# Turning rows by VectorE and a DRAM scratch in a conditioned transformer block, and moving weight splits and film products by some steps

## The chip, the cores and the metric

The kernel runs on one core of a Trainium2 chip. The time is that of the device for one execution, in microseconds (us), and lower is better. The core has TensorE (PE, matmuls), VectorE (DVE), ScalarE (ACT), GpSimd (POOL) and SyncE (SP, which only issues DMA transfers here). Each engine works through its own instruction queue in order, and the queues meet only at semaphores.

## The reference

The block has 2 batches of 1024 tokens with 256 features, all in fp32:

```python
def rmsnorm(x, w):
    return x * rsqrt(mean(x * x, -1) + 1e-6) * w
def film(x, cond, w, b):
    scale, shift = split(cond @ w + b, 2)
    return x * (1 + scale) + shift
h = film(rmsnorm(x, norm1_w), cond, film1_w, film1_b)
Q, K, V = h @ q_w + q_b, h @ k_w + k_b, h @ v_w + v_b
x = x + softmax(Q K^T / 16) V @ proj_w + proj_b
h = film(rmsnorm(x, norm2_w), cond, film2_w, film2_b)
return x + gelu(h @ mlp_w1 + mlp_b1) @ mlp_w2 + mlp_b2      # hidden width 1024
```

## The kernel before

**Tiles and groups.** The 2048 tokens are 16 tiles of 128; four tiles are a group, 0 to 3. Rows (`x_rows`) lie with a token per partition. A product needs its left side with a feature per partition; those are the columns `hT`. Each fp32 value is split in a high part (fp32r) and a low part (what is left), and each product is made in three passes (low x high, high x low, high x high). Whatever TensorE multiplies therefore has a high half, made by ScalarE or GpSimd, and a low half, made by VectorE.

**Phase 1** (to about 45 us) loads, makes the first norm and film, turns the rows of each group and makes `G_all` (queries with the key weights folded in) and `V_all` (values with the output projection folded in).

**Phase 2** is attention, one tile a step, `for t in range(TILES)` on each engine. In step t TensorE makes `scores(t)` and then `attention(t - 4)` (`LAG` is 4). VectorE takes the row maximum (L590), turns the probabilities in 32x32 blocks (`turn_blocks`, L601), takes the low half of turned probabilities of tile t - 3 (`crossed_lo`, L608), adds the result of attention to the rows (`add_attention`, L617), and in steps 4 to 11 makes one product for the second film (`film_products`, L477) with the other operand, the condition row, beside it; four products end in `coefficients` (L486, L489) for one batch. ScalarE takes the exponential (`exp`, L386), issues the store of the turned probabilities to a DRAM scratch (`store_turned`, L405) and casts the high half of what came back (`crossed_hi`, L397). SP issues the four loads that bring each tile back with its blocks crossed (L226). `crossed_hi(t)`, then `crossed_lo(t)`, then `attention(t)` is a fixed chain. GpSimd, once `crossed_lo(t)` is done, adds the output bias to the rows of tile t (L305), splits MLP weights (`split_weights`, L292 and L294, one eighth at a time), and adds the second bias (L299).

**The second norm of a group**: squares on ScalarE (`squares_after`, L412), the inverse root on GpSimd (`inverse_rms`, L253 and L256), normed rows on VectorE (`normed_rows`, L497, into `xn`), eight 128x128 transposes on TensorE (`transpose_rows`, L697), film on ScalarE out of PSUM (`columns`, L344), high half on GpSimd (`high_columns`, L261), low half on VectorE (`low_columns`, L511). For group 0 this lies in phase 2.

**Phase 3** is the MLP, one group after the other, eight steps m each: TensorE makes the hidden block m (`hidden`, L705) and the second product of block m - 2 (`project_hidden`, L820); ScalarE takes gelu twice, in fp32 and in fp32r (`gelu_tile`, L446); VectorE takes the low half (`gelu_low`, L653). `finished_rows` (L672) adds the result to the rows, and SP stores them (L234). The transposes for group g + 1 stand in step 4 of group g. The first four hidden blocks of group 0 (`EARLY`) are mixed with the last attentions. Groups 1 and 2 run in a hardware loop (`Fori`) on TensorE, ScalarE and VectorE.

The order is written out by hand in each engine's part, and where the phases meet, ScalarE has this one:

```python
store_turned(TILES - 1)
crossed_hi(TILES - 3)
gelu_tile(0, 0, False)
gelu_tile(0, 1, False)
crossed_hi(TILES - 2)
gelu_tile(0, 2, False)
crossed_hi(TILES - 1)
gelu_tile(0, 3, False)
squares_after(1)
```

## Time and profile before

| | us |
|---|---|
| median of 3 runs (lowest, highest) | 234.83 (233.73, 235.23) |
| the profiled execution | 234.44 |
| its span in the trace | 232.6 |
| TensorE busy in it | 219.7 (94%) |
| VectorE, ScalarE, GpSimd busy | 144.1, 110.7, 71.1 |

The profiled execution's own time is 1.8 us longer than the span from its first to its last instruction. Times in rows count from the span's start. A busy time is a mean over phases: VectorE's 62% is made of a phase 2 that is nearly full and a phase 3 that is not.

### The profile page before, as it was taken

The numbers are of one execution on the slowest core, as the hardware profiler recorded it, in microseconds if no ns is written. First come the engines' busy times: TensorE is split into PE (matmuls) and PEld (weight loads), VectorE is DVE, ScalarE is ACT, GpSimd is POOL, SyncE is SP. The second block draws the span as 40 slices with busy tenths as digits, with TensorE's granted clock in tenths as the row PEclk, the third lists the DMA queues.
The fourth block names the chain that finished last, engine by engine and source line by source line (L and its number), as shares of the span: only waits on it lengthen the run. The fifth ranks groups of instructions, "written<-read, shape, count | busy, mean of one in ns | idle before, by whom it ended". The sixth has DMA issues, their size and how long they took to land.

```text
span 232.6 us, 3855 instructions
## 1 busy us (share of the span) xinstructions
PE 219.7 (94%) x1380; PEld 196.0 (84%) x1380; DVE 144.1 (62%) x276; ACT 110.7 (48%) x207; POOL 71.1 (31%) x102
## 2 busy tenths in 40 slices
PE   0998999999979999999999899999999999999994
PEld 0767988978769999999999799999999999999994
DVE  0599767669599999999879564143524352433223
ACT  3158654425333355423472970367436743644440
POOL 1575851003325513743343224221232123200000
PEclk9999999999999999999999999999999999999999
DMA  6994000054568967665575410000200020002002
GB/s 167 342 368 209 3 19 28 3 180 147 191 222 240 280 215 245 215 211 166 165 239 181 154 30 0 3 0 0 93 0 0 0 90 0 0 4 90 0 3 90
DMA packets 15713, 26.72 MB, mean 115 GB/s; under 512 B 1872, under 2 KB 10064, under 8 KB 15568
## 3 DMA queue, kind: packets, MB, share of 16 engines
q1 hardware_dynamic: 13392, 18.11, 25.2%
q10 hardware_dynamic: 2304, 8.39, 9.4%
q8 instruction: 10, 0.16, 0.3%
q14 instruction: 7, 0.06, 0.1%
HBM read 16.00 MB, written 10.49 MB: 114 GB/s over the span
## 4 chain that ended last, share of the span: by engine, by line
PE 78%; DVE 9%; DMA 6%; issue 2%; SPq 2%; ACT 1%; ACTq 0%; DVEq 0%
PE psum L705 36%; PE psum L820 20%; PE psum L779 16%; DMA raw<-in_film_wT_dram 3%; PE psum L723 3%; DMA crossing<-raw 2%; PE psum L697 2%; PE psum L717 2%; DVE hT L511 1%; DMA keys_first<-crossing 1%; ACT probsT L397 1%; SPq L189 1%; DVE probsT L608 1%; DVE raw L601 1%; DVE V_all L504 1%
## 5 line engine op out<-in xcount | busy, mean ns | idle before, releaser
L653 DVE TENSOR_TENSOR G_all<-probs,G_all 128x512 fp32r<-128x512 f32 x32 | 22.7, 711 | 51.6 <-ACT G_all L446 51.6
L779 PEld LDWEIGHTS psum<-V_all,probsT 128*128 128x128 f32 x384 | 47.1, 188 | 5.1 <-DVE probsT L608 4.2
L820 PEld LDWEIGHTS psum<-w,G_all 128*128 128x128 f32 x384 | 49.6, 191 | 2.1
L820 PE MATMUL psum<-w,G_all 128*128 128x256 f32 x384 | 50.9, 283 | 0.0
L779 PE MATMUL psum<-V_all,probsT 128*128 128x256 f32 x384 | 48.3, 282 | 2.5 <-DVE probsT L608 2.4
L705 PE MATMUL psum<-hT,w 128*128 128x512 f32 (+1 forms) x192 | 49.3, 393 | 0.0
L705 PE MATMUL psum<-hT,G_all 128*128 128x512 f32 x192 | 46.6, 393 | 0.1
L446 ACT ACTIVATE probs<-psum,vcol 128x512 f32<-128x512 f32 x32 | 22.0, 688 | 45.1 <-PE psum L705 45.1
L705 PEld LDWEIGHTS psum<-hT,G_all 128*128 128x128 f32 x192 | 35.1, 188 | 7.7 <-ACT probs L386 0.6
L705 PEld LDWEIGHTS psum<-hT,w 128*128 128x128 f32 x192 | 34.1, 189 | 5.8
L397 ACT CAST probsT<-keys_first 128x1024 fp32r<-128x1024 f32 x16 | 16.8, 1052 | 41.3 <-DVE raw L601 16.6
L305 POOL TENSOR_TENSOR x_rows<-x_rows,add_row 128x256 f32<-128x256 f32 x16 | 11.8, 738 | 69.0 <-DVE probsT L608 69.0
L608 DVE TENSOR_TENSOR probsT<-keys_first,probsT 128x1024 fp32r<-128x1024 f32 x16 | 19.6, 1223 | 6.1 <-ACT probsT L397 5.4
L590 DVE TENSOR_REDUCE row_max<-psum 128x1 f32<-128x1024 f32 x16 | 19.2, 1200 | 5.1 <-PE psum L705 5.1
L446 ACT ACTIVATE G_all<-psum,vcol 128x512 fp32r<-128x512 f32 x32 | 21.9, 683 | 0.0
L386 ACT ACTIVATE probs<-psum,exp_bias 128x1024 f32<-128x1024 f32 x16 | 17.9, 1119 | 7.5 <-DVE exp_bias L593 7.5
L261 POOL TENSOR_SCALAR hT<-h_full 128x512 fp32r<-128x512 f32 x16 | 11.3, 711 | 23.5 <-ACT h_full L344 23.2
L299 POOL TENSOR_TENSOR x_rows<-x_rows,add_row 128x256 f32<-128x256 f32 x16 | 12.9, 828 | 11.1 <-DVE xn L497 11.1
L511 DVE TENSOR_TENSOR hT<-h_full,hT 128x512 fp32r<-128x512 f32 (+1 forms) x16 | 11.4, 744 | 3.0 <-POOL hT L261 3.0
L705 PE MATMUL psum<-probsT,hT 128*128 128x258 f32 x96 | 12.4, 285 | 0.0
L344 ACT ACTIVATE h_full<-psum,coef 128x512 f32<-128x512 f32 x16 | 11.6, 778 | 1.8 <-DVE coef L489 1.2
L705 PEld LDWEIGHTS psum<-probsT,hT 128*128 128x128 f32 x96 | 11.9, 189 | 0.1
(63 smaller groups left out, 198.7 us busy)
## 6 DMA issues: line engine op xcount, KB each, us to landing
keys_first<-crossing SPq DMA_DIRECT2D x64, 128.0 KB, 3.0
crossing<-turned ACTq DMA_DIRECT2D x8, 512.0 KB, 4.1
crossing<-raw ACTq DMA_DIRECT2D x8, 512.0 KB, 3.4
out_dram<-x_rows SPq DMA_DIRECT2D x8, 256.0 KB, 2.1
x_rows<-in_x_dram SPq DMA_DIRECT2D x3, 512.0 KB, 9.4
raw<-in_film_wT_dram SPq DMA_DIRECT2D x2, 512.0 KB, 8.5
raw<-in_mlp_w_dram SPq DMA_DIRECT2D x1, 1024.0 KB, 7.6
raw<-in_mlp_w_dram SPq DMA_DIRECT2D x4, 256.0 KB, 4.6
```

What stands on the lines that cost most here:

```text
L299: pool.tensor_tensor(row, row, add_row[:, 1, :], ALU.add).then_inc(bias2_added, 1)
L305: pool.tensor_tensor(x_rows[:, t, :], x_rows[:, t, :], add_row[:, 0, :], ALU.add).then_inc(residual_ready, 1)
L386: act.activation(probs[:, parity, :], psum[:, 2 * parity:2 * parity + 2, :].rearrange("p a n -> p (a n)"), ACT.Exp, bias=exp_bias[:, t:t + ...
L397: act.copy(probsT[:, t % 2, HI, :, :].rearrange("p k (a n) -> p k a n", n=Q), keys_first[:, t % 2, :, :, :].rearrange("p a k n -> p k a n" ...
L446: act.activation(dst, bank(2 + m % 2), ACT.Gelu, bias=vcol[:, B1 + m:B1 + m + 1]).then_inc(gelu_done, 1)
L511: dve.tensor_tensor(hT[:, LO, d, tokens], h_full[:, d, :], hT[:, HI, d, tokens].bitcast(F32), ALU.subtract).then_inc(h_ready, 1)
L590: dve.reduce_max(row_max[:, col], psum[:, 2 * parity:2 * parity + 2, :].rearrange("p a n -> p (a n)"), AX_X, negate=True).then_inc(max_don ...
L608: dve.tensor_tensor(lo, keys_first[:, t % 2, :, :, :].rearrange("p a k n -> p k a n"), hi.bitcast(F32), ALU.subtract).then_inc(probsT_read ...
L653: dve.tensor_tensor(gelu[:, m, LO, :], gelu_full[:, m % 2, :], gelu[:, m, HI, :].bitcast(F32), ALU.subtract).then_inc(gelu_ready, 1)
L705: last = pe.matmul(dst, stationary(a, k), moving(b, k), start=(n == len(tiles) * len(PASSES) - 1), stop=(n == 0))
L779: last = pe.matmul(bank(6 + t % 2, D), probsT[:, t % 2, a, k, :], V_all[:, t // KT * KT + k, s, :], start=(n == 0), stop=(n == KT * len(PA ...
L820: last = pe.matmul(bank(4 + j, D), gelu[:, m, a, j * P:(j + 1) * P], w2[:, b, m, :], start=(m == 0 and n == 0), stop=(m == HT - 1 and n == ...
```

## The change

1. **Rows of groups 1 to 3 are turned without TensorE.** A new `turn_rows(g)` on VectorE turns `xn` in 32x32 blocks into `turned_rows`. `cross_rows(g)` on SP stores this 512 KB to the scratch `rows_crossing` and loads it back in four pieces with the blocks crossed, into `columns_first`. ScalarE's `columns_after` reads that instead of PSUM. Group 0 is turned by TensorE as before.
2. **The places of this work.** The squares of group 1 stand right behind ScalarE's last `store_turned`; norm and turn of group 1 stand on VectorE ahead of `crossed_lo(15)`. Those of groups 2 and 3 are in step 0 of the group before, ahead of `finished_rows`, with the squares in step 6 of the group before that.
3. **The weight splits** on GpSimd go from steps 0 to 3 and 6 to 9 to steps 4 to 7 and 10 to 13, and SP's loads of the second weights from steps 5 to 8 to steps 9 to 12. `turned_rows` and `columns_first` lie in the memory of the raw weights. TensorE waits for four pieces ahead of its first hidden block and for all eight ahead of the rest.
4. **The film products** on VectorE go from steps 4 to 11 to steps 5 to 8 (one each), 9 and 10 (two each).
5. The `Fori` loops of phase 3 are written out.

```diff
+        rows_crossing = nc.dram_tensor("rows_crossing", [GROUPS, P, GT * D], F32)
...
+        turned_rows = raw[:, 0:GT * D]
+        columns_first = raw[:, GT * D:2 * GT * D].rearrange("p (a d j n) -> p a d j n", a=QT, d=DT, j=GT)
...
+        rows_turned, rows_out, columns_in = sem("rows_turned"), sem("rows_out"), sem("columns_in")
...
             for t in range(TILES):
-                if 5 <= t < 9:
-                    sp.wait_ge(mlp_ready, t - 4)
-                    load(w2_raw[:, (t - 5) * 512:(t - 4) * 512].rearrange("p (t n) -> p t n", n=D),
-                         mlp_w2[:, (t - 5) * 2:(t - 4) * 2, :], w2_in[t - 5])
+                if 9 <= t < 13:
+                    sp.wait_ge(mlp_ready, t - 8)
+                    load(w2_raw[:, (t - 9) * 512:(t - 8) * 512].rearrange("p (t n) -> p t n", n=D),
+                         mlp_w2[:, (t - 9) * 2:(t - 8) * 2, :], w2_in[t - 9])
                 sp.wait_ge(turned_out, 16 * (t + 1))
...
-            with sp.Fori(0, B) as b:
-                for t in range(0, KT, 2):
-                    sp.wait_ge(rows_done, b * KT + (TILES + t + 2))
-                    sp.dma_start(out_v[:, ds(b, 1), t:t + 2, :].rearrange("p b t n -> p (b t) n"),
-                                 x_rows[:, ds(b * KT + t, 2), :]).then_inc(stored, 16)
+            def cross_rows(g):
+                sp.wait_ge(rows_turned, g)
+                sp.dma_start(rows_crossing[g, :, :], turned_rows).then_inc(rows_out, 16)
+                sp.wait_ge(rows_out, 16 * g)
+                sp.wait_ge(h_done, DT * (GROUPS + g))
+                for q in range(QT):
+                    sp.dma_start(
+                        columns_first[q * Q:(q + 1) * Q, :, :, :, :].rearrange("p a d j n -> p a (d j n)"),
+                        rows_crossing[g, :, q * GT * DT * Q:(q + 1) * GT * DT * Q].rearrange("(a p) n -> p a n", p=Q),
+                    ).then_inc(columns_in, 16)
+
+            def store_rows(g):
+                b, first = divmod(g * GT, KT)
+                for j in range(0, GT, 2):
+                    sp.wait_ge(rows_done, TILES + g * GT + j + 2)
+                    sp.dma_start(out_v[:, b, first + j:first + j + 2, :],
+                                 x_rows[:, g * GT + j:g * GT + j + 2, :]).then_inc(stored, 16)
+
+            cross_rows(1)
+            cross_rows(2)
+            store_rows(0)
+            cross_rows(3)
+            for g in range(1, GROUPS):
+                store_rows(g)
             sp.wait_ge(stored, 16 * TILES // 2)

         @block.gpsimd
...
-                    pool.wait_ge(w2_in[t - 6], 16)
-                    split_weights(w2_raw, w2_flat, t - 6, 4)
+                if 4 <= t < 8:
+                    split_weights(w1_raw, w1_flat, t - 4, 0)
+                if 10 <= t < 14:
+                    pool.wait_ge(w2_in[t - 10], 16)
+                    split_weights(w2_raw, w2_flat, t - 10, 4)
                 if t == 6:
...
@@ -318,9 +341,12 @@
                     second_bias(t - 10)
                 if t == 11:
                     high_columns(GROUPS, 0)
+                if t == 13:
+                    inverse_rms(GROUPS + 1)

             for g in range(1, GROUPS):
-                inverse_rms(g + GROUPS)
+                if g > 1:
+                    inverse_rms(g + GROUPS)
                 pool.wait_ge(xn_done, TILES + GT * (g + 1))
                 for j in range(GT):
...
@@ -407,16 +433,27 @@
             def squares_after(g, tiles=range(GT), place=lambda j: xn[:, j, :]):

                 act.wait_ge(rows_done, g * GT + GT)
-                act.wait_ge(xT_done, g + GROUPS)
+                if g <= 1:
+                    act.wait_ge(xT_done, g + GROUPS)
+                else:
+                    act.wait_ge(rows_turned, g - 1)
                 for j in tiles:
                     last = act.activation(place(j), x_rows[:, ds(g * GT + j, 1), :].rearrange("p t n -> p (t n)"),
                                           ACT.Square, accum_out=sumsq[:, ds(g * GT + (TILES + j), 1)])
                 if GT - 1 in tiles:
                     last.then_inc(sq_done, 1)

-            def columns_after(g, first=0):
+            def columns_after(g):
                 act.wait_ge(h_ready, g * DT + DT * GROUPS)
-                columns(g + GROUPS, 1, ds(g // 2, 1), first)
+                if g == 0:
+                    columns(GROUPS, 1, slice(0, 1), 4)
+                else:
+                    act.wait_ge(columns_in, 16 * QT * g)
+                    for d in range(DT):
+                        act.activation(h_full[:, d, :].rearrange("p (j a n) -> p j a n", j=GT, a=QT),
+                                       columns_first[:, :, d, :, :].rearrange("p a j n -> p j a n"), ACT.Identity,
+                                       bias=coef[:, 1, g // 2, DT + d:DT + d + 1],
+                                       scale=coef[:, 1, g // 2, d:d + 1]).then_inc(h_done, 1)

             squares_place = [h_full[:, 0, D:2 * D], h_full[:, 1, 0:D], h_full[:, 1, D:2 * D], xn[:, GT - 1, :]]
             high_V(GROUPS - 1, range(2))
...
@@ -447,6 +484,7 @@
                                    ).then_inc(gelu_done, 1)

             store_turned(TILES - 1)
...
@@ -454,20 +492,17 @@
             gelu_tile(0, 2, False)
             crossed_hi(TILES - 1)
             gelu_tile(0, 3, False)
-            squares_after(1)
-
-            def mlp(g, before, more):
-                for m in range(0 if before else EARLY, HT):
-                    gelu_tile(g, m, before)
-                    if more and m == 0:
-                        squares_after(g + 1)
-                    if more and m == 5:
+
+            def mlp(g):
+                for m in range(0 if g else EARLY, HT):
+                    gelu_tile(g, m, g > 0)
+                    if m == 5 and g + 1 < GROUPS:
                         columns_after(g + 1)
-
-            mlp(0, False, True)
-            with act.Fori(1, GROUPS - 1) as g:
-                mlp(g, True, True)
-            mlp(GROUPS - 1, True, False)
+                    if m == 6 and g + 2 < GROUPS:
+                        squares_after(g + 2)
+
+            for g in range(GROUPS):
+                mlp(g)

         @block.vector
...
+
+            def turn_rows(g):
+
+                dve.wait_ge(xn_done, TILES + GT * (g + 1))
+                dve.wait_ge(mlp_ready, 8)
+                if g > 1:
+                    dve.wait_ge(rows_out, 16 * (g - 1))
+                dve.transpose(turned_rows.rearrange("p (q d j n) -> p d j q n", q=QT, d=DT, j=GT),
+                              xn[:, :, :].rearrange("p j (d q n) -> p d j q n", d=DT, q=QT)).then_inc(rows_turned, 1)

...
                     add_attention(t - LAG)
-                if LAG <= t < LAG + 2 * DT * B:
-                    b, k = divmod(t - LAG, 2 * DT)
-                    if t == LAG:
+                if 5 <= t < 9:
+                    if t == 5:
                         dve.wait_ge(film_in[1], 16)
                         dve.wait_ge(wide_in, 32)
-                    film_products(1, b, lambda n: h_full[:, 0, 0:D], (k,))
-                    if k == 2 * DT - 1:
-                        coefficients(1, b)
+                    film_products(1, 0, lambda n: h_full[:, 0, 0:D], (t - 5,))
+                    if t == 8:
+                        coefficients(1, 0)
+                if t in (9, 10):
+                    film_products(1, 1, lambda n: xn[:, 2, :] if n % 2 else h_full[:, 0, 0:D], (2 * t - 18, 2 * t - 17))
+                    if t == 10:
+                        coefficients(1, 1)
                 if t in (TILES - 5, TILES - 4):
                     normed_rows(GROUPS, 0, range(2) if t == TILES - 5 else range(2, GT))
...
@@ -658,11 +705,12 @@
             crossed_lo(TILES - 2)
             add_attention(TILES - 3)
             gelu_low(0, 2)
+            normed_rows(GROUPS + 1, GT)
+            turn_rows(1)
             crossed_lo(TILES - 1)
             add_attention(TILES - 2)
             gelu_low(0, 3)
             add_attention(TILES - 1)
-            normed_rows(GROUPS + 1, GT)

             def finished_rows(g):
                 for j in range(GT):
...
+                        normed_rows(g + (GROUPS + 1), g * GT + GT)
+                        turn_rows(g + 1)
+                    if m == 0:
                         finished_rows(g - 1)
-                    if more and m == 2:
-                        normed_rows(g + (GROUPS + 1), g * GT + GT)
-                    if more and m == 6:
-                        low_columns(g + (GROUPS + 1), ds(g * GW + GW, GW))
-
-            mlp(0, False, True)
-            with dve.Fori(1, GROUPS - 1) as g:
-                mlp(g, True, True)
-            mlp(GROUPS - 1, True, False)
+                    if m == 6 and g + 1 < GROUPS:
+                        low_columns(g + (GROUPS + 1), slice(g * GW + GW, g * GW + 2 * GW))
+
+            for g in range(GROUPS):
+                mlp(g)
             finished_rows(GROUPS - 1)

...
@@ -822,22 +869,20 @@
                     if m == HT - 1:
                         last.then_inc(mlp_done, 1)

-            def mlp(g, before, more):
+            def mlp(g, before):

...
-                    if more and m == 4:
-                        transpose_rows(g + (GROUPS + 1))
                     if m >= 2:
                         project_hidden(g, m - 2, before)
                     elif before:
                         project_hidden(g - 1, HT - 2 + m)

             attention(TILES - 4)
-            pe.wait_ge(mlp_ready, 8)
+            pe.wait_ge(mlp_ready, 4)
...
@@ -847,10 +892,9 @@
             hidden(0, 3)
             attention(TILES - 2)
             attention(TILES - 1)
-            mlp(0, False, True)
...
-            mlp(GROUPS - 1, True, False)
+            pe.wait_ge(mlp_ready, 8)
+            for g in range(GROUPS):
+                mlp(g, g > 0)
             for m in (HT - 2, HT - 1):
                 project_hidden(GROUPS - 1, m)


```

**ScalarE where phase 2 ends.** The `DMA` row is the store of turned probabilities of tile 15, `CAST` is `crossed_hi`, first of tile 13, `ACTIVATE xn,sumsq` is a square. Before:

```order
L405 DMA crossing<-raw 128x1024 [waits turned_out,blocks_turned]
L397 CAST probsT<-keys_first 128x1024 [waits attn_done,keys_in_odd]
L446 ACT_TABLE_LOAD [waits blocks_turned]
L446 ACTIVATE probs<-psum,vcol 128x512 [waits hidden_done]
L446 ACTIVATE G_all<-psum,vcol 128x512
...
L397 CAST probsT<-keys_first 128x1024 [waits attn_done,keys_in_odd]
L446 ACTIVATE probs<-psum,vcol 128x512 [waits gelu_ready,hidden_done]
L446 ACTIVATE G_all<-psum,vcol 128x512
L412 ACTIVATE xn,sumsq<-x_rows 128x256 [waits xT_done,rows_done]
```

Now:

```order
L431 DMA crossing<-raw 128x1024 [waits turned_out,blocks_turned]
L441 ACTIVATE xn,sumsq<-x_rows 128x256 [waits xT_done,rows_done]
L441 ACTIVATE xn,sumsq<-x_rows 128x256 x3
L423 CAST probsT<-keys_first 128x1024 [waits attn_done,keys_in_odd]
L483 ACT_TABLE_LOAD [waits blocks_turned]
L483 ACTIVATE probs<-psum,vcol 128x512 [waits hidden_done]
L483 ACTIVATE G_all<-psum,vcol 128x512
```

The squares have gone from behind the fourth gelu to ahead of the cast of tile 13 and of all four gelus.

**VectorE at the same meeting of phases.** `probsT<-keys_first,probsT` is `crossed_lo`, here of tile 15, `G_all` is `gelu_low`, `xn<-x_rows` the normed rows of group 1. Before:

```order
L653 TENSOR_TENSOR G_all<-probs,G_all 128x512 [waits gelu_done]
L608 TENSOR_TENSOR probsT<-keys_first,probsT 128x1024 [waits probsT_hi]
L614 RECIPROCAL row_inv<-row_sum 128x1 [waits attn_done]
L617 SCALAR_TENSOR_TENSOR x_rows<-psum,row_inv,x_rows 128x256 [waits residual_ready,inv_done]
L653 TENSOR_TENSOR G_all<-probs,G_all 128x512 [waits gelu_done]
L614 RECIPROCAL row_inv<-row_sum 128x1 [waits attn_done]
L617 SCALAR_TENSOR_TENSOR x_rows<-psum,row_inv,x_rows 128x256 [waits residual_ready,inv_done]
L497 TENSOR_SCALAR xn<-x_rows,rstd 128x256 [waits rstd_done]
L497 TENSOR_SCALAR xn<-x_rows,rstd 128x256 x3
L653 TENSOR_TENSOR G_all<-probs,G_all 128x512 [waits gelu_done] x3
```

Now:

```order
L700 TENSOR_TENSOR G_all<-probs,G_all 128x512 [waits gelu_done]
L532 TENSOR_SCALAR xn<-x_rows,rstd 128x256 [waits rstd_done]
L532 TENSOR_SCALAR xn<-x_rows,rstd 128x256 x3
L541 STREAM_TRANSPOSE raw<-xn 128x8x4x32 [waits mlp_ready,xn_done]
L652 TENSOR_TENSOR probsT<-keys_first,probsT 128x1024 [waits probsT_hi]
L658 RECIPROCAL row_inv<-row_sum 128x1 [waits attn_done]
L661 SCALAR_TENSOR_TENSOR x_rows<-psum,row_inv,x_rows 128x256 [waits residual_ready,inv_done]
L700 TENSOR_TENSOR G_all<-probs,G_all 128x512 [waits gelu_done]
L658 RECIPROCAL row_inv<-row_sum 128x1 [waits attn_done]
L661 SCALAR_TENSOR_TENSOR x_rows<-psum,row_inv,x_rows 128x256 [waits residual_ready,inv_done]
```

The normed rows have gone from behind the last `add_attention` to ahead of `crossed_lo(15)`, and the new turn of `xn` stands between.

**VectorE in step 10.** `h_full,film_sum<-raw,xn` is a film product, followed by the read of its sum. Before:

```order
L614 RECIPROCAL row_inv<-row_sum 128x1 [waits attn_done]
L617 SCALAR_TENSOR_TENSOR x_rows<-psum,row_inv,x_rows 128x256 [waits residual_ready,inv_done]
L477 ISA h_full,film_sum<-raw,xn 128x256
L477 ISA film_sum 128x1
L601 STREAM_TRANSPOSE turned<-probs 128x8x4x32 [waits turned_out,exp_done]
L590 TENSOR_REDUCE row_max<-psum 128x1 [waits scores_done]
```

Now:

```order
L658 RECIPROCAL row_inv<-row_sum 128x1 [waits attn_done]
L661 SCALAR_TENSOR_TENSOR x_rows<-psum,row_inv,x_rows 128x256 [waits residual_ready,inv_done]
L512 ISA h_full,film_sum<-raw,xn 128x256
L512 ISA film_sum 128x1
L512 ISA xn,film_sum<-raw,xn 128x256
L512 ISA film_sum 128x1
L521 TENSOR_TENSOR coef<-film_sum,vcol 128x4 [waits film_sums]
L524 SCALAR_TENSOR_TENSOR coef<-coef,vcol 128x2 [waits shift_ready]
L645 STREAM_TRANSPOSE turned<-probs 128x8x4x32 [waits turned_out,exp_done]
L634 TENSOR_REDUCE row_max<-psum 128x1 [waits scores_done]
```

Where one product stood there are two, with the coefficients of the second batch behind them, all ahead of the turn of tile 10.

## Rows read from the trace of the kernel before

**Rows 1.** The page: engines, busy; a gelu pass: count, busy, mean ns.

```profile
PE 219.7 (94%) x1380; PEld 196.0 (84%) x1380; DVE 144.1 (62%) x276; ACT 110.7 (48%) x207; POOL 71.1 (31%) x102
...
L446 ACT ACTIVATE probs<-psum,vcol 128x512 f32<-128x512 f32 x32 | 22.0, 688 | 45.1 <-PE psum L705 45.1
```

**Rows 2.** Chain of waits, whole span: start us, length us, what.

```profile
63.69 3.14 DMA crossing<-raw
...
109.27 2.84 PE psum L779 x24
...
130.65 3.11 PE psum L779 x24
...
136.52 5.68 PE psum L779 x48
...
146.46 0.87 PE psum L697 x8
...
193.34 0.87 PE psum L697 x8
```

**Rows 3.** Timeline, TensorE (PE), 60 to 232.6 us: start, length, instruction [idle before <-releaser].

```profile
103.49 3.00 PE L779 MATMUL psum<-V_all,probsT 128*128 128x256 f32 x24
...
130.65 3.11 PE L779 MATMUL psum<-V_all,probsT 128*128 128x256 f32 x24 [0.65 <-DVE probsT L608]
...
164.09 1.60 PE L820 MATMUL psum<-w,G_all 128*128 128x256 f32 x12
```

**Rows 4.** Timeline, ScalarE (ACT), 96 to 175 us.

```profile
127.86 0.33 ACTq L405 DMA_DIRECT2D crossing<-raw  x1
128.28 1.05 ACT L397 CAST probsT<-keys_first 128x1024 fp32r<-128x1024 f32 x1 [4.10 <-DVE raw L601]
...
138.43 0.43 ACT L412 ACTIVATE xn<-x_rows 128x256 f32<-128x256 f32 x1
...
139.62 0.42 ACT L412 ACTIVATE xn<-x_rows 128x256 f32<-128x256 f32 x1
```

**Rows 5.** Timeline, VectorE (DVE), 96 to 175 us.

```profile
126.59 1.23 DVE L601 STREAM_TRANSPOSE raw<-probs 128x1024 f32<-128x1024 f32 x1
129.37 1.23 DVE L608 TENSOR_TENSOR probsT<-keys_first,probsT 128x1024 fp32r<-128x1024 f32 x1 [1.54 <-ACT probsT L397]
...
137.41 1.23 DVE L608 TENSOR_TENSOR probsT<-keys_first,probsT 128x1024 fp32r<-128x1024 f32 x1 [0.24 <-ACT probsT L397]
...
142.83 1.14 DVE L497 TENSOR_SCALAR xn<-x_rows,rstd 128x256 f32<-128x256 f32 x4
```

**Rows 6.** Timeline, VectorE, 60 to 110 us.

```profile
64.14 1.43 DVE L477 CUSTOM_DVE_ANT_0 h_full<-raw,xn 128x256 f32<-128x256 f32 x1
...
96.12 0.58 DVE L477 CUSTOM_DVE_ANT_0 h_full<-raw,xn 128x256 f32<-128x256 f32 x1
...
98.08 1.23 DVE L590 TENSOR_REDUCE row_max<-psum 128x1 f32<-128x1024 f32 x1 [0.20 <-PE psum L705]
...
99.53 1.22 DVE L608 TENSOR_TENSOR probsT<-keys_first,probsT 128x1024 fp32r<-128x1024 f32 x1
...
101.97 0.45 DVE L486 TENSOR_TENSOR coef<-film_sum,vcol 128x4 f32<-128x4 f32 x1
```

**Rows 7.** Timeline, GpSimd (POOL), 50 to 110 us.

```profile
63.99 1.30 POOL L294 TENSOR_TENSOR w<-raw,w 128x512 fp32r<-128x512 f32 x1
...
96.40 0.80 POOL L292 TENSOR_SCALAR w<-raw 128x512 fp32r<-128x512 f32 x1
97.28 1.30 POOL L294 TENSOR_TENSOR w<-raw,w 128x512 fp32r<-128x512 f32 x1
```

**Rows 8.** Timeline, VectorE, 160 to 175 us.

```profile
161.94 1.50 DVE L672 TENSOR_TENSOR x_rows<-psum,x_rows 128x256 f32 x4 [1.20 <-PE psum L820]
```

**Rows 9.** The page: DMA issues, count, KB each, median us to landing.

```profile
keys_first<-crossing SPq DMA_DIRECT2D x64, 128.0 KB, 3.0
...
crossing<-raw ACTq DMA_DIRECT2D x8, 512.0 KB, 3.4
```

14 lines of the change are left out of this document (5 added, 9 removed).

## The prediction

> **What bounds the kernel now.** I read the page first: TensorE is busy 94% of the span, VectorE 62%, the others less [rows 1]. Then the chain of waits: from 69.7 us to 229.6 us it stays on TensorE but for one piece, around 125 to 130 us. There attention of the fourteenth tile (tile 13) starts after 0.65 us of idle time, released by VectorE's low half of the turned probabilities (L608) [rows 2, 3]. A stretch of eight 128x128 transposes stands in that chain with 0.87 us each time; those for groups 1 and 3 are at 146.46 and 193.34 [rows 2], with group 2's midway. So whatever leaves TensorE's queue after 70 us is a gain, provided its queue never waits for a new reason. VectorE matters next: between 50 and 100 us it has almost no gap, and it hands TensorE one tile at a time.
>
> The profiled execution took 234.44 us (span 232.6). The median of the shown runs is 234.83. My sums are against 234.44, 0.4 us under that median, which is small beside the terms.
>
> **Term 1, the transposes of groups 1 to 3.** 3 x 0.87 = **-2.6 us**, all of it on the path. TensorE now also waits for all eight weight pieces only after attention of tile 15, and for four before its first hidden matmul. By rows the first four are split by about 100 us; nothing is won or lost by it.
>
> **Term 2, the squares of group 1 on ScalarE.** Four Square instructions, 0.40 us apart (138.43 to 140.0) [rows 4], stand today behind the last early gelu, where ScalarE has time. Now they stand right behind ScalarE's last store of turned rows and ahead of the cast of tile 13 (L397). What is queued behind them is the critical piece: VectorE's turn ends at 127.8, ScalarE issues the store at 127.86, casts at 128.28, VectorE takes the low half at 129.37, TensorE starts at 130.65 [rows 3 to 5]. ScalarE is in order and is idle before 127.86, waiting for that turn, so the squares cannot run earlier. The cast moves to 129.88 and TensorE's wait grows from 0.65 to 2.25: **+1.6 us**. Bounds: 1.5 to 1.7, since the same instructions were timed.
>
> **Term 3, norm and turn of group 1 on VectorE.** Its four row products (1.14) [rows 5] and a new 32x32 block turn of 128x1024 now stand ahead of the low half of tile 15. The turn has the shape of today's L601, 1.23 [rows 5]. Together 2.37. Today that low half runs at 137.41 to 138.64, after 0.24 idle, and attention of tile 15 starts 2.84 into the 48 matmuls at 136.52, that is 139.36: slack 0.72 [rows 2, 5]. Everything here has moved by the 1.6 of term 2 alike, so the slack stays. 2.37 less 0.24, less some 0.1 by which neighbours overlap, gives 2.0; less 0.72 is 1.3 us of stall. A restart of TensorE costs more: attention takes 3.11 after a wait and 2.84 without [rows 2], 0.27. Together **+1.6 us**. The products need the inverse norm from GpSimd, which now has in step 13 a residual, a weight split (0.7 to 0.8 and 1.30 [rows 7]), a bias and the two norm instructions: by today's durations it is done between 137 and 139.4, wanted at 138.7. So the bounds are 1.0 (half the overlap I assume is missing) and 2.5 (norm 0.7 late and slow).
>
> **Term 4, film products on VectorE.** The eight move from steps 4 to 11 to steps 5 to 8 (one each), 9 and 10 (two each). Step 4 loses one of 1.43 us [rows 6]; nothing comes of it, because ScalarE next needs the store issued at 63.69 to land at 66.83 [rows 2] before it can go on. Step 11 loses its product, its coefficients and their quarrel with GpSimd. The price lies in steps 9 and 10. A product runs today at 96.12 beside GpSimd's residual and ends at 96.70; GpSimd's L292 has then begun and ends at 97.20, L294 (1.30) follows [rows 6, 7]. The trace shows that such pairs exclude each other: the product issued at 64.14 took 1.43 where another took 0.58, because L294 was in progress since 63.99, and it ended 0.28 after L294 [rows 6, 7]. The second product, issued at 96.65 in these terms, waits to 97.20, ends at about 97.5: 0.86 more than today. Twice that, 1.7. The coefficients leave step 7 (-0.4), come to step 8 (+0.7, as at 101.97, where the first took 0.45 [rows 6]) and to step 10, where the first would find L294 in progress: 1.4, or 0.4 if it slips in. Less the 0.2 that VectorE idles before 98.08, the maximum of tile 11 is 3.3 us later (2.3 if it slips in). TensorE bears 2.7: attention of tile 8 starts at 103.49, its low half ends today at 100.75 [rows 3, 6]. So the stall is 0.6 plus 0.27 for the restart, **+0.8 us**; the lower bound is 0. Steps 11 and 12 then have only two row products each and step 13 nothing added, so I take VectorE to be abreast again by step 14, as it was at 98.08.
>
> What the notes add: the Trainium skill ("SBUF — State Buffer", Who interferes with whom) says that a VectorE instruction with two SBUF inputs and a GpSimd instruction that reads SBUF exclude each other for the whole instruction, whichever issues first going first. That is what the product at 64.14 shows (1.43 instead of 0.58). The rule does not say who goes next when both wait; read with L294 issued first it would make term 4 3.4 in place of 0.8, which is rival (c) below.
>
> **At nothing.** The weight splits, 2 us each on GpSimd, go from steps 0 to 3 and 6 to 9 to steps 4 to 7 and 10 to 13. GpSimd idles several us a step there. The high columns of group 0 come some 2 us later behind a split, at about 123.3, and VectorE wants them at 124.84; if that cover were gone, each us late would be a us of TensorE. The round trip of a group through DRAM: store 3.4, four loads issued in 1.7 and landed 3.0 later [rows 9], together some 8 us, plus the turn. A step of the MLP is (46.88 - 2 x 0.87) / 16 = 2.82, from the transposes of groups 1 and 3 [rows 2]. In times of today's group 1, VectorE is free at 160.74 (161.94 less 1.20), so norm and turn of group 2 end at 163.1 [rows 8]. ScalarE wants the columns behind its gelu of the sixth hidden block, whose matmuls end three steps after 164.09, at 172.5, and two passes of 0.69 later it is 173.9 [rows 1, 3]. The columns are there at 163.1 + 8.1 = 171.2: 2.7 us of cover, and the same for group 3. Group 1 has about 4. SP issues these ahead of the output stores, which nobody waits for but the last. In the same place VectorE's finished rows (1.50 for four) come behind norm and turn: they would start at about 163.1 in place of 161.94 and end at 164.6, and TensorE needs the first at 164.09 and the last 1.1 later [rows 3, 8]: just in time, zero, up to 0.3 each. The loops written out cost and save nothing, as TensorE shows no gap at them.
>
> **Sum.** -2.6 + 1.6 + 1.6 + 0.8 = +1.4, so **235.8 us**. With the bounds of terms 3 and 4 the forecast's own range is 234.4 to 236.8.
>
> **Rivals.**
> (a) The change simply gains: the tail waits are hidden, and the time is 234.4 - 2.6 = 231.8. For it: TensorE is the bound nearly everywhere. Against it: [rows 3 to 5] show no slack before tile 13's cast, and ScalarE is in order. 10%.
> (b) Only one of the two tail waits counts and VectorE holds its pace: -2.6 + 1.6 + 0 to 0.8, that is 233.4 to 234.2. It needs the low half of tile 15 to find 2 us of cover that I do not see, or none of term 4. 17%.
> (c) Slower: the shared access of VectorE and GpSimd. If L294 goes ahead of the second product in steps 9 and 10, each costs 1.3 more. The maximum of tile 11 is then 5.9 late instead of 3.3, and TensorE waits 3.1 + 0.27. Decisive point: that maximum later than 100.8. The sum is -2.6 + 1.6 + 1.6 + 3.4 = +4.0, 238.4. For it: L294 is issued 0.08 after L292 ends [rows 7]. Against it: in today's rows the one that waited went next. 14%.
> (d) The change doesn't deliver: the round trip takes twice its 8 us beside other transfers, the columns come 5 us late in groups 2 and 3, and TensorE, which has one step of 2.8 in hand, loses 2.5 in each: 241. The DMA queues are nearly empty there, so 4%.
> The forecast has the remaining 55%.
>
> **How the numbers follow.** A measurement of this kernel tells about 1% from no change, 2.3 us. Faster by more than that is (a) and the very edge of (b): 0.12. Slower is (c), (d) and a little of the forecast's upper end: 0.20. The rest, 0.68, is within 1%. The range 233.0 to 238.2 leaves out (a), (d) and the upper part of (c).
>
> **What the changed profile would show.** Term 1: no L697 transposes of groups 1 to 3, and TensorE without a gap from about 146 us to the end. Term 2: four squares between the last store and the cast of tile 13, and an idle of about 2.2 us before that attention. Term 3: an idle of 1 to 2 us before attention of tile 15, released by VectorE's low half. Term 4: second film products of about 0.9 and a small idle near 104 us. I am wrong if TensorE shows no idle time between 120 and 146 us beyond today's, or waits inside the MLP groups for columns or finished rows.

## The result, and the profile after

| | before | after |
|---|---|---|
| median, us (4 runs each) | 235.03 (233.73 to 235.58) | 237.57 (236.92 to 238.21) |
| profiled execution, us | 234.44 | 237.56 |
| its span, us | 232.6 | 235.5 |

The ratio is 1.0100, with a 95% interval of 1.0063 to 1.0137: slower, by about the 1% that a measurement of this kernel can tell. Three of the four executions of the changed kernel, the profiled one among them, had a mean granted TensorE clock of 0.993 and spans of 235.5 to 235.6 us. The fourth had 1.000 and 234.2. The forecast span was 232.6 + 1.4 = 234.0.

In the experiments below the medians and the counts of executions are of all of them, and the ratios leave out one of e1_squares_first (237.75) and one of s1_before_squares_late (239.68), each over 1.5% longer than the fastest of its kernel.

The page of the changed kernel: engines, busy time, and the DMA issues of the new round trip. TensorE has 24 matmuls less than in [rows 1].

```profile
PE 219.0 (93%) x1356; PEld 194.6 (83%) x1356; DVE 148.4 (63%) x279; ACT 110.8 (47%) x207; POOL 73.1 (31%) x102
...
rows_crossing<-raw SPq DMA_DIRECT2D x3, 512.0 KB, 2.6
raw<-rows_crossing SPq DMA_DIRECT2D x12, 128.0 KB, 2.9
```

The timeline of TensorE in the changed kernel, as in [rows 3]: start, length, instruction, idle time before it with its releaser. L826 is attention, L752 the hidden matmuls, L867 the projections.

```profile
98.20 3.00 PE L826 MATMUL psum<-V_all,probsT 128*128 128x256 f32 x24
...
109.63 3.00 PE L826 MATMUL psum<-V_all,probsT 128*128 128x256 f32 x24
...
124.97 3.11 PE L826 MATMUL psum<-V_all,probsT 128*128 128x256 f32 x24 [0.24 <-DVE probsT L652]
127.91 2.94 PE L752 MATMUL psum<-hT,w 128*128 128x512 f32 x12
133.24 4.62 PE L826 MATMUL psum<-V_all,probsT 128*128 128x256 f32 x24 [2.38 <-DVE probsT L652]
137.70 2.93 PE L752 MATMUL psum<-hT,w 128*128 128x512 f32 x12
140.47 3.00 PE L826 MATMUL psum<-V_all,probsT 128*128 128x256 f32 x24
144.77 3.11 PE L826 MATMUL psum<-V_all,probsT 128*128 128x256 f32 x24 [1.31 <-DVE probsT L652]
147.72 2.55 PE L867 MATMUL psum<-w,G_all 128*128 128x256 f32 x20
...
228.11 4.47 PE L867 MATMUL psum<-w,G_all 128*128 128x256 f32 x36
```

The waits before tile 13 (2.38) and tile 15 (1.31) are the two that terms 2 and 3 forecast. The third thing to see is the length 4.62 at 133.24: the same 24 matmuls took 3.11 after a wait before [rows 3].

The same stretch of the changed kernel in windows of 1 us; the third figure from the right is the granted clock, ahead of DMA share and GB/s.

```profile
133.00:134.00 1.00, 0.76 (x4) 0.77 (x5) 0.74 (x3) 0.99 (x3) 0.74 (x2) 0.76 0.00 0
134.00:135.00 1.00, 1.00 (x7) 1.00 (x6) 0.46 (x1) 1.00 (x3) 0.92 (x2) 0.50 0.46 134
...
136.00:137.00 1.00, 1.00 (x7) 1.00 (x7) 1.00 (x2) 0.59 (x1) 1.00 (x2) 0.54 0.52 118
137.00:138.00 1.00, 1.00 (x10) 0.95 (x9) 1.00 (x1) 0.00 (x0) 0.92 (x2) 1.00 0.00 0
```

TensorE was idle from 130.85 to 133.24. The granted clock then stands at 0.50, its 1.2 GHz level, from about 133.5 to 136.9, with 7 matmuls a microsecond in place of 10.

Starts on TensorE before and after, in the order of time, give the whole shift. The last column is what the prediction had for the same stretch.

| TensorE reaches | before | after | shift | new here | forecast here |
|---|---|---|---|---|---|
| attention of tile 7 | 97.88 | 98.20 | +0.32 | +0.32 | 0 |
| attention of tile 9 | 109.10 | 109.63 | +0.53 | +0.21 | +0.8 (term 4) |
| hidden block 0 of group 0 | 127.07 | 127.91 | +0.84 | +0.31 | 0 ("at nothing") |
| attention of tile 13 | 130.65 | 133.24 | +2.59 | +1.75 | +1.6 (term 2) |
| hidden block 2 | 133.59 | 137.70 | +4.11 | +1.52 | 0 |
| attention of tile 14 | 136.36 | 140.47 | +4.11 | 0 | 0 |
| first projection | 142.03 | 147.72 | +5.69 | +1.58 | +1.6 (term 3) |
| last 36 matmuls | 225.07 | 228.11 | +3.04 | -2.65 | -2.6 (term 1) |

The first +0.32 stands in the trace from 56 us on, ahead of everything that the prediction costs. s1_before_squares_late below, whose code is that of before up to 128 us, reaches its hidden block 0 at 127.40, 0.33 late as well, so I take it for the scatter of executions.

ScalarE of the changed kernel, to be read against [rows 4]: the four squares (L441) between the last store and the cast of tile 13 (L423).

```profile
128.85 0.33 ACTq L431 DMA_DIRECT2D crossing<-raw  x1
129.28 0.42 ACT L441 ACTIVATE xn<-x_rows 128x256 f32<-128x256 f32 x1 [4.57 <-DVE raw L645]
...
130.50 0.40 ACT L441 ACTIVATE xn<-x_rows 128x256 f32<-128x256 f32 x1
...
130.90 1.03 ACT L423 CAST probsT<-keys_first 128x1024 fp32r<-128x1024 f32 x1
```

The cast starts 1.62 after the place that the first square took.

VectorE of the changed kernel, against [rows 5, 6]: film products (L512), coefficients (L521), the maximum of tile 11 (L634), low halves (L652), low columns (L555), low half of a gelu (L700), norm (L532) and turn (L541) of group 1.

```profile
91.96 0.82 DVE L512 CUSTOM_DVE_ANT_0 xn<-raw,xn 128x256 f32<-128x256 f32 x1
...
98.62 1.12 DVE L521 TENSOR_TENSOR coef<-film_sum,vcol 128x4 f32<-128x4 f32 x1
...
101.03 1.18 DVE L634 TENSOR_REDUCE row_max<-psum 128x1 f32<-128x1024 f32 x1
...
123.38 1.53 DVE L652 TENSOR_TENSOR probsT<-keys_first,probsT 128x1024 fp32r<-128x1024 f32 x1
...
125.42 2.24 DVE L555 TENSOR_TENSOR hT<-h_full,hT 128x512 fp32r<-128x512 f32 x2
...
131.96 1.23 DVE L652 TENSOR_TENSOR probsT<-keys_first,probsT 128x1024 fp32r<-128x1024 f32 x1 [3.14 <-ACT probsT L423]
...
135.69 1.23 DVE L700 TENSOR_TENSOR G_all<-probs,G_all 128x512 fp32r<-128x512 f32 x1 [0.47 <-ACT G_all L483]
136.84 1.75 DVE L652 TENSOR_TENSOR probsT<-keys_first,probsT 128x1024 fp32r<-128x1024 f32 x1
...
141.19 1.14 DVE L532 TENSOR_SCALAR xn<-x_rows,rstd 128x256 f32<-128x256 f32 x4
142.37 1.25 DVE L541 STREAM_TRANSPOSE raw<-xn 128x1024 f32<-128x1024 f32 x1
143.53 1.18 DVE L652 TENSOR_TENSOR probsT<-keys_first,probsT 128x1024 fp32r<-128x1024 f32 x1
```

And GpSimd of the changed kernel beside it, as in [rows 7]: high columns (L284), second halves of weight splits (L317) and an addition of the second bias (L322).

```profile
92.59 1.34 POOL L317 TENSOR_TENSOR w<-raw,w 128x512 fp32r<-128x512 f32 x1
...
121.27 1.29 POOL L317 TENSOR_TENSOR w<-raw,w 128x512 fp32r<-128x512 f32 x1
...
123.22 2.17 POOL L284 TENSOR_SCALAR hT<-h_full 128x512 fp32r<-128x512 f32 x2
...
127.21 1.61 POOL L317 TENSOR_TENSOR w<-raw,w 128x512 fp32r<-128x512 f32 x1
...
134.66 1.71 POOL L317 TENSOR_TENSOR w<-raw,w 128x512 fp32r<-128x512 f32 x1
136.33 1.18 POOL L322 TENSOR_TENSOR x_rows<-x_rows,add_row 128x256 f32<-128x256 f32 x1
```

The low half of 1.53 in place of 1.23 stands where GpSimd runs its high columns. At 134.66 the split runs beside a gelu's low half, which takes 1.23 in place of 0.69, and the bias addition that the split has pushed back runs beside the low half of 1.75. Both sides are slowed: L317 takes 1.61 beside the low columns and 1.71 beside the gelu, 1.29 at 121.27, and L322 takes 1.18 in place of 0.74.

### The profile page after: what moved, and what is told of

Same layout as the page of the kernel before. It is cut to its first block, busy times and chain, and to the rows that moved or that the text cites. A ratio compares the mean times of both kernels' runs of the same rounds, so it can differ in the third digit from the quotient of the medians.

```text
span 235.5 us, 3657 instructions
## 1 busy us (share of the span) xinstructions
PE 219.0 (93%) x1356; PEld 194.6 (83%) x1356; DVE 148.4 (63%) x279; ACT 110.8 (47%) x207; POOL 73.1 (31%) x102
## 4 chain that ended last, share of the span: by engine, by line
PE 74%; DVE 11%; DMA 7%; issue 3%; ACT 2%; SPq 2%; ACTq 0%; DVEq 0%
PE psum L752 35%; PE psum L867 19%; PE psum L826 14%; DMA raw<-in_film_wT_dram 3%; PE psum L770 2%; DMA crossing<-raw 2%; DVE probsT L652 2%; PE psum L764 1%; DMA keys_first<-crossing 1%; ACT probsT L423 1%; DVE hT L555 1%; PE psum L744 1%; SPq L193 1%; DVE row_max L634 1%; DVE raw L645 1%
## 5 line engine op out<-in xcount | busy, mean ns | idle before, releaser
L826 PEld LDWEIGHTS psum<-V_all,probsT 128*128 128x128 f32 x384 | 48.6, 194 | 9.0 <-DVE probsT L652 8.3
L826 PE MATMUL psum<-V_all,probsT 128*128 128x256 f32 x384 | 50.2, 288 | 5.8 <-DVE probsT L652 5.8
L700 DVE TENSOR_TENSOR G_all<-probs,G_all 128x512 fp32r<-128x512 f32 x32 | 23.4, 730 | 51.0 <-ACT G_all L483 51.0
L867 PEld LDWEIGHTS psum<-w,G_all 128*128 128x128 f32 x384 | 49.8, 191 | 2.3
L867 PE MATMUL psum<-w,G_all 128*128 128x256 f32 x384 | 50.6, 283 | 0.0
L752 PE MATMUL psum<-hT,w 128*128 128x512 f32 x192 | 49.3, 393 | 0.0
L752 PE MATMUL psum<-hT,G_all 128*128 128x512 f32 x192 | 46.5, 393 | 0.1
L752 PEld LDWEIGHTS psum<-hT,G_all 128*128 128x128 f32 x192 | 35.1, 188 | 7.6 <-ACT probs L412 0.6
L752 PEld LDWEIGHTS psum<-hT,w 128*128 128x128 f32 x192 | 34.1, 189 | 5.8
L423 ACT CAST probsT<-keys_first 128x1024 fp32r<-128x1024 f32 x16 | 16.8, 1049 | 38.8 <-DMA keys_first<-crossing 10.6
L328 POOL TENSOR_TENSOR x_rows<-x_rows,add_row 128x256 f32<-128x256 f32 x16 | 11.8, 739 | 70.7 <-DVE probsT L652 70.7
L652 DVE TENSOR_TENSOR probsT<-keys_first,probsT 128x1024 fp32r<-128x1024 f32 x16 | 20.4, 1275 | 9.1 <-ACT probsT L423 8.4
L284 POOL TENSOR_SCALAR hT<-h_full 128x512 fp32r<-128x512 f32 x16 | 12.2, 768 | 37.4 <-ACT h_full L453 28.7
L634 DVE TENSOR_REDUCE row_max<-psum 128x1 f32<-128x1024 f32 x16 | 19.2, 1198 | 4.4 <-PE psum L752 4.4
L322 POOL TENSOR_TENSOR x_rows<-x_rows,add_row 128x256 f32<-128x256 f32 x16 | 12.3, 793 | 8.8 <-DVE xn L532 8.8
L555 DVE TENSOR_TENSOR hT<-h_full,hT 128x512 fp32r<-128x512 f32 x16 | 11.8, 769 | 3.0 <-POOL hT L284 3.0
L752 PE MATMUL psum<-probsT,hT 128*128 128x258 f32 x96 | 12.4, 285 | 0.0
L752 PEld LDWEIGHTS psum<-probsT,hT 128*128 128x128 f32 x96 | 11.9, 189 | 0.1
L317 POOL TENSOR_TENSOR w<-raw,w 128x512 fp32r<-128x512 f32 x8 | 11.1, 1394 | 0.7
```

The source lines that it names most:

```text
L284: pool.tensor_scalar(hT[:, HI, d, g * GW:(g + 1) * GW], h_full[:, d, :], 1.0, 0.0, ALU.mult, ALU.add).then_inc(h_hi, 1)
L322: pool.tensor_tensor(row, row, add_row[:, 1, :], ALU.add).then_inc(bias2_added, 1)
L423: act.copy(probsT[:, t % 2, HI, :, :].rearrange("p k (a n) -> p k a n", n=Q), keys_first[:, t % 2, :, :, :].rearrange("p a k n -> p k a n" ...
L555: dve.tensor_tensor(hT[:, LO, d, tokens], h_full[:, d, :], hT[:, HI, d, tokens].bitcast(F32), ALU.subtract).then_inc(h_ready, 1)
L634: dve.reduce_max(row_max[:, col], psum[:, 2 * parity:2 * parity + 2, :].rearrange("p a n -> p (a n)"), AX_X, negate=True).then_inc(max_don ...
L652: dve.tensor_tensor(lo, keys_first[:, t % 2, :, :, :].rearrange("p a k n -> p k a n"), hi.bitcast(F32), ALU.subtract).then_inc(probsT_read ...
```

## The experiments

Ten kernels, each timed against the kernel before in turn on one chip: e1, e2, e3 and s1 together (before 234.68), f1, f3, s2 and e4 together (235.13), f2 and e5 together (235.11). All of them compute the whole reference. Diffs are against the kernel named.

**Squares ahead of the last store (e1_squares_first, from after).**

```diff
-            store_turned(TILES - 1)
             squares_after(1)
+            store_turned(TILES - 1)
             crossed_hi(TILES - 3)
```

> The changed kernel with one swap: on ScalarE the four squares of group 1 stand ahead of the last store of turned rows instead of behind it, that is in the 4 us in which ScalarE waits for VectorE's turn anyway. Theory (term 2): the wait of TensorE before attention of tile 13 falls from 2.38 to about 0.8 us, and the fall of the granted clock behind it (that attention took 4.62 instead of 3.11 us) goes too; the changed kernel loses 3.1 us, to about 234.4. Rival A (the loss comes from the moved weight splits and film products, which make VectorE late): the cast still comes late and less than 1 us returns. Rival B (the clock falls for a reason other than this wait): 1.6 us return and that attention still takes over 4 us.

Measured: 235.69 (12 runs), ratio 1.0022 [0.9998, 1.0046]. TensorE's timeline:

```profile
131.45 3.10 PE L826 MATMUL psum<-V_all,probsT 128*128 128x256 f32 x24 [0.79 <-DVE probsT L652]
...
142.08 4.63 PE L826 MATMUL psum<-V_all,probsT 128*128 128x256 f32 x24 [1.96 <-DVE probsT L652]
```

The squares ran at 124.6 to 126.2, where ScalarE waits for VectorE's turn anyway, and the wait before tile 13 fell from 2.38 to 0.79. So term 2 is the place of the squares; 0.14 of that wait is something else. By the medians 1.9 us came back, where 3.1 was expected. The wait before tile 15 became 1.96, not 1.31, and now that attention took 4.63. Windows of this kernel across it:

```profile
140.00:142.00 2.00, 0.12 (x2) 0.00 (x0) 2.00 (x3) 0.00 (x0) 0.00 (x0) 1.00 0.12 49
142.00:146.00 4.00, 3.92 (x20) 3.92 (x21) 1.35 (x4) 0.00 (x0) 3.89 (x5) 0.57 0.53 186
```

In the profiled execution the drop of the clock moved with the long wait, from tile 13 to tile 15.

**The squares alone, in the kernel before (s1_before_squares_late, from before).**

```diff
             store_turned(TILES - 1)
+            squares_after(1)
             crossed_hi(TILES - 3)
...
             gelu_tile(0, 3, False)
-            squares_after(1)
```

> The kernel before, with only this moved: the squares of group 1 on ScalarE stand behind the last store of turned rows, ahead of the cast of tile 13, as in the changed kernel. Theory (term 2 with the clock): TensorE's wait there grows from 0.65 to 2.25 us and the attention behind it takes about 4.6 us: 3.1 us slower than before, about 238. Rival B: 1.6 us slower, with that attention at 3.1 us.

Measured: 236.94 (6 runs), ratio 1.0071 [1.0047, 1.0096], 1.7 us. TensorE:

```profile
132.57 4.62 PE L779 MATMUL psum<-V_all,probsT 128*128 128x256 f32 x24 [2.25 <-DVE probsT L608]
```

The wait is the 2.25 of term 2, to the hundredth, and nothing of the rest of the change is in this kernel. The 1.7 us are by the ratio; the median of all six executions is 2.3 over that of before. The profiled execution has the lower clock behind the wait (mean 0.991, span 236.1), and the longest of the others has a low mean clock too (0.990, span 237.9); the remaining four have not (0.997 to 0.999, spans 234.2 to 235.7). So the time is 1.6 for the wait, and the sum of wait and clock that I had expected is reached by those two executions, not by the ratio.

**Half of the squares late (s2_two_squares_late, from before).**

```diff
+            squares_after(1, range(2))
             store_turned(TILES - 1)
+            squares_after(1, range(2, GT))
             crossed_hi(TILES - 3)
```

> The kernel before, with two of the four squares of group 1 ahead of ScalarE's last store and two behind it, ahead of the cast of tile 13. Theory: the wait of TensorE there is 0.65 + 0.8 = 1.45 us, 0.8 us slower than before, and the granted clock holds, so the attention behind it takes 3.1 us. Rival E (any wait over 1 us costs the clock): that attention takes about 4.6 us and the kernel is 2.3 us slower.

Measured: 235.98 (10 runs), ratio 1.0030 [1.0013, 1.0047], 0.7 us.

```profile
132.51 3.11 PE L780 MATMUL psum<-V_all,probsT 128*128 128x256 f32 x24 [1.47 <-DVE probsT L609]
```

Two squares add 0.82 to the 0.65 and leave attention at 3.11. The mean clock was 0.997 or more in all ten executions. The cost of squares in front of the cast is linear, 0.4 each.

**e1 with the weight splits and their loads back in the steps of before (f3_e1_old_splits, from e1).**

```diff
-                if 4 <= t < 8:
-                    split_weights(w1_raw, w1_flat, t - 4, 0)
-                if 10 <= t < 14:
-                    pool.wait_ge(w2_in[t - 10], 16)
-                    split_weights(w2_raw, w2_flat, t - 10, 4)
+                if t < 4:
+                    split_weights(w1_raw, w1_flat, t, 0)
+                if 6 <= t < 10:
+                    pool.wait_ge(w2_in[t - 6], 16)
+                    split_weights(w2_raw, w2_flat, t - 6, 4)
```

SP's loads of w2 go back from tiles 9 to 12 to tiles 5 to 8 in the same way.

> The kernel of e1 (squares in ScalarE's idle time) with the weight splits and loads back in their old steps. Theory (GpSimd's share of term 3): in e1 the low half of tile 14 took 1.75 and the normed rows 1.61 us beside GpSimd's split and norm, against 1.23 and 1.14 without; both go, and the wait at tile 15 falls from 1.96 to 1.2 or 1.3 us, near the 1.3 of the prediction. With it the clock holds in more executions. Median 1.5 to 2 us under e1. Rival: the wait stays at 1.9 and so does the time.

Measured: 234.22 (12 runs), ratio 0.9966 [0.9950, 0.9982]. TensorE, then VectorE in the same trace:

```profile
104.26 3.11 PE L826 MATMUL psum<-V_all,probsT 128*128 128x256 f32 x24 [0.52 <-DVE probsT L652]
...
131.49 3.10 PE L826 MATMUL psum<-V_all,probsT 128*128 128x256 f32 x24 [0.65 <-DVE probsT L652]
...
141.50 3.11 PE L826 MATMUL psum<-V_all,probsT 128*128 128x256 f32 x24 [1.31 <-DVE probsT L652]
```

```profile
134.88 1.23 DVE L652 TENSOR_TENSOR probsT<-keys_first,probsT 128x1024 fp32r<-128x1024 f32 x1 [0.24 <-ACT probsT L423]
...
137.93 1.14 DVE L532 TENSOR_SCALAR xn<-x_rows,rstd 128x256 f32<-128x256 f32 x4
```

With the split gone the low half is at 1.23 again, and the wait at tile 15 is the 1.3 that term 3 worked out from norm and turn alone. e1's other 0.65 came with the split of step 13 and what it pushed back on GpSimd: there the gelu's low half took 1.24, the low half of tile 14 1.75 beside the bias addition, and the normed rows 1.61, against 0.69, 1.23 and 1.14 here. The clock was 0.998 or more in all 12 executions. By the ratios the gain on e1 is 1.3 us, where 1.5 to 2 was expected.

**Only the splits back (f1_only_old_splits, from after).** The same edit, with after's squares:

```diff
-                if 4 <= t < 8:
+                if t < 4:
...
-                if 10 <= t < 14:
+                if 6 <= t < 10:
```

> The changed kernel with only the weight splits and the loads of the second weights back in the steps of the kernel before. Theory (GpSimd's reads hold up VectorE in steps 12 to 15): the wait of 0.24 at tile 12 goes (0.5 us with its restart), the two low columns take 1.8 instead of 2.24, so the cast of tile 13 is 0.4 earlier by itself; the squares stay in front of it, so the wait there stays at 2.2 us. 0.5 to 1.0 us faster than the changed kernel. Rival A: 2 us or more.

Measured: 236.81 (4 runs), ratio 1.0075 [1.0052, 1.0098]; 0.8 under after, with intervals that overlap. TensorE's rows:

```profile
127.35 2.92 PE L752 MATMUL psum<-hT,w 128*128 128x512 f32 x12
132.52 3.11 PE L826 MATMUL psum<-V_all,probsT 128*128 128x256 f32 x24 [2.25 <-DVE probsT L652]
```

The wait at tile 12 is gone. The hidden block starts 0.56 earlier than in after, but 0.25 of that stands ahead of tile 11 already (121.48 against 121.73), so 0.31 came back with the wait, which is the table's +0.31. The wait at tile 13 is 2.25 again. This profiled execution kept the clock (1.000, span 233.3); the three others had 0.993 and 234.8 to 235.3. One kernel, two kinds of execution, some 1.5 to 2 us apart.

**Only the film products back (f2_only_old_film, from after).**

```diff
-                if 5 <= t < 9:
...
-                if t in (9, 10):
...
+                if LAG <= t < LAG + 2 * DT * B:
+                    b, k = divmod(t - LAG, 2 * DT)
```

> The changed kernel with only the film products back in steps 4 to 11, one each. Theory (term 4 is 0.2 us, as the first trace after the change shows at tile 8): 0.1 to 0.4 us faster than the changed kernel, the waits at tiles 13 and 15 as they are. Rival A (VectorE's load of steps 9 and 10 is the main loss): over 1 us faster.

Measured: 236.98 (5 runs), ratio 1.0079 [1.0049, 1.0109]. Beside after's interval this tells nothing apart; waits of 2.02 and 1.92 at tiles 13 and 15, and a clock of 0.993 in three of five executions. What term 4 cost shows in the traces better than in the times. From attention of tile 7 to that of tile 9 TensorE took:

| film products | us from tile 7 to tile 9 |
|---|---|
| old steps: before, f2, e3, e4, e5, s1 | 11.21 to 11.23 |
| old steps: s2 | 11.69 |
| new steps: after, e1, e2, f1, f3 | 11.43, 11.48, 11.49, 11.59, 11.99 |

So the new steps cost 0.2 to 0.4 in four executions and 0.8 in f3. s2 has 0.5 there without them: ScalarE's cast waited for the loads from DRAM until 100.44. The old steps can be late by chance, but only the new ones are late every time.

**Norm and turn behind the last early gelu (e2_norm_behind, from e1).**

```diff
-            normed_rows(GROUPS + 1, GT)
-            turn_rows(1)
             crossed_lo(TILES - 1)
             add_attention(TILES - 2)
             gelu_low(0, 3)
+            normed_rows(GROUPS + 1, GT)
+            turn_rows(1)
             add_attention(TILES - 1)
```

> The swap of e1, and on VectorE norm and turn of group 1 moved from ahead of the low half of tile 15 to behind the low half of the fourth gelu. Theory (term 3): TensorE's wait of 1.31 us before attention of tile 15 goes with its restart, another 1.6 us, so about 232.8. The turned rows leave about 2 us later and their columns still come in time. Rival C (the low half of tile 15 would be late anyway, by the keys from DRAM): under 0.4 us returns. Rival D (columns late): a new wait of TensorE at the first hidden block of group 1.

Measured: 233.34 (5 runs), ratio 0.9928 [0.9907, 0.9948]. The wait before tile 15 is gone and one of 0.36 is new, in the first projection, released by VectorE's `add_attention`, which now stands behind the turn. Both tail waits taken away, the change gains.

**The old splits and film products as well (e3_old_splits, from e2).** The edits of f3 and f2 together:

```diff
-                if 4 <= t < 8:
+                if t < 4:
...
-                if 5 <= t < 9:
+                if LAG <= t < LAG + 2 * DT * B:
```

> e2, with weight splits, loads of the second weights and film products in the steps of the kernel before. What is left of the change is the turn by VectorE and DRAM for groups 1 to 3. Theory: the stall of 0.2 at tile 8 and that of 0.24 at tile 12 (its low half, 1.53 instead of 1.23, beside GpSimd's high columns) go with their restarts, 0.5 to 0.8 us, so about 232.1, 2.6 to 2.9 us under the kernel before. Rival A would have it 2 us faster than e2.

Measured: 233.19 (6 runs), ratio 0.9931 [0.9905, 0.9957]. The wait at tile 12 is gone and tile 13's is 0.65, and the profiled span is 0.8 shorter (230.7 against 231.5), but the medians differ by 0.15 and the ratios not at all. The gain I expected is not there in the times.

**The turn behind the last attention sum (e4_turn_last, from e3).**

```diff
             normed_rows(GROUPS + 1, GT)
-            turn_rows(1)
             add_attention(TILES - 1)
+            turn_rows(1)
```

> The kernel of e3 with one swap on VectorE: the addition of attention of tile 15 stands between the norm and the turn of group 1 instead of behind both. Theory: the last small wait of TensorE there (0.37 us and its restart, released by that addition) goes, 0.4 us, so 0.2% faster than e3; the columns of group 1 come 1.1 us later and are still in time. Rival D (columns late): ScalarE waits for them, and TensorE has a new wait of up to 1 us before the first hidden block of group 1.

Measured: 233.10 (6 runs), ratio 0.9915 [0.9888, 0.9942]. The wait in the first projection went and another came:

```profile
156.73 1.65 PE L749 MATMUL psum<-hT,w 128*128 128x512 f32 x6 [0.25 <-DVE hT L555]
```

The columns of group 1, whose turn starts at 142.96 instead of 142.04 in e3, now miss the first hidden block of group 1: rival (d) in small, at the one group that the prediction gave about 4 us of cover.

**Norm and turn each in a gap (e5_norm_in_gap, from e4).** The norm goes behind the turn of tile 15, where VectorE waits for ScalarE's cast (1.54 of idle, [rows 5]), and the turn ahead of the last sum. GpSimd's inverse norm of group 1 comes at step 12.

```diff
-                if t == 13:
+                if t == 12:
                     inverse_rms(GROUPS + 1)
...
+            normed_rows(GROUPS + 1, GT)
             crossed_lo(TILES - 3)
...
             gelu_low(0, 3)
-            normed_rows(GROUPS + 1, GT)
-            add_attention(TILES - 1)
             turn_rows(1)
+            add_attention(TILES - 1)
```

> The kernel of e4 with norm and turn of group 1 in gaps of VectorE: the inverse norm on GpSimd one step earlier, the four row products behind the turn of tile 15, where VectorE waits 1.5 us for ScalarE's cast, and the turn of the rows ahead of the last addition, where it waits again. Theory: all of it is covered, the columns come 1 us earlier than in e4 and its wait of 0.3 us at the first hidden block of group 1 goes, so 0.2 to 0.4 us under e4, about 2.6 us under the kernel before. Rival F (the row products don't fit: GpSimd's norm is late): VectorE waits ahead of the low half of tile 13 and TensorE's wait there grows from 0.65 towards 1.5 us.

Measured: 232.02 (6 runs, 231.81 to 232.37), ratio 0.9868 [0.9845, 0.9892]. VectorE, then TensorE:

```profile
126.92 1.23 DVE L645 STREAM_TRANSPOSE raw<-probs 128x1024 f32<-128x1024 f32 x1
128.19 1.14 DVE L532 TENSOR_SCALAR xn<-x_rows,rstd 128x256 f32<-128x256 f32 x4
129.69 1.23 DVE L652 TENSOR_TENSOR probsT<-keys_first,probsT 128x1024 fp32r<-128x1024 f32 x1 [0.35 <-ACT probsT L423]
...
140.94 1.23 DVE L541 STREAM_TRANSPOSE raw<-xn 128x1024 f32<-128x1024 f32 x1
```

```profile
130.97 3.11 PE L823 MATMUL psum<-V_all,probsT 128*128 128x256 f32 x24 [0.67 <-DVE probsT L652]
...
136.65 5.84 PE L823 MATMUL psum<-V_all,probsT 128*128 128x256 f32 x48
...
222.73 4.47 PE L864 MATMUL psum<-w,G_all 128*128 128x256 f32 x36
```

The norm fills 1.14 of the idle time and the low half still waits 0.35 for the cast. TensorE waits 0.67, as before the change, and has no wait behind it. The last matmuls start at 222.73, 2.34 before those of before: term 1 with nothing given back but the scatter. It is the fastest of all kernels here, 1.3% under the kernel before and 2.3% under the change as made (0.9868 / 1.0100).

## Why the prediction was right, and where it fell short

It forecast +1.4 us, and the medians are 2.5 apart: 237.57 lies inside the stated range of 233.0 to 238.2, but 0.8 above the 236.8 that the bounds of its own terms allowed. It is also nearer to rival (c)'s 238.4 than to the forecast of 235.8, though (c)'s mechanism did not act. So the direction and the three new costs were foreseen, the clock's share was not, and that the time fell inside the range owes something to the width that was left for (c). The terms:

- **Term 1, -2.6: right.** 2.65 between the first projection and the last 36 matmuls, and e5 shows it by itself.
- **Term 2, +1.6: right as to cause and size.** s1 holds nothing but these squares and has the wait of 2.25, s2 has half of it, e1 takes it away. After has 0.13 more; its low columns took 2.24 beside GpSimd, 1.83 in f1.
- **What term 2 lacked is what stood behind the wait.** The prediction gave a wait its own length and 0.27 for the restart. At tile 13 attention itself took 4.62 instead of 3.11, with the granted clock at 0.50: +1.52 in the profiled execution, the largest miss, and most of the 1.8 us between forecast and median. What a fall costs in the end is nearer 1.4: after's spans are 235.5 to 235.6 with it and 234.2 in the one execution without, where the sum gives 234.0.
- **Term 3, +1.6: right as to cause, and in its size two misses cancel.** f3 shows norm and turn by themselves: a wait of 1.31, and 0.27 of restart. Beside the split of step 13, with the clock kept, the wait is 1.96 (e1) or 1.92 (f2): 0.6 that I did not have. In after's profiled execution 1.31 stands there again: VectorE stood idle 1.39 before 140.59, until the late hidden block and its gelu were done, so the slow attention of tile 13 hid the delay. The norm from GpSimd, my upper bound, was not last in after: it ended at 139.77 and the normed rows started at 141.19. In e1 it was level with VectorE: it ended at 138.00, the gelu's low half at 138.02, and the rows started at 138.03.
- **Term 4, +0.8: right as to cause, mis-sized; it was 0.2 in after.** Each second product kept VectorE 0.75 (91.96 to 92.71) where I had 0.86, and the first coefficient instruction 1.12 where I had 1.4 or 0.4. With the 0.32 of the whole trace taken off, the maximum of tile 11 was 2.6 later, between my 2.3 and 3.3, and TensorE bears 2.7. But the margin is thin: the same instructions made that maximum 3.2 late against TensorE in f3, and there the wait was 0.52 and the price 0.8, as forecast. VectorE had less lead there before the first product of step 10 (97.57 with tile 7's attention at 97.98; 97.24 and 98.20 in after), and why is open.
- **"At nothing" failed in one place: the high columns of group 0.** I looked at when they would be ready for VectorE's low columns and put that at 123.3, 1.5 us early. Pushed behind the split they only began at 123.22, beside VectorE's low half of tile 12. The two took 2.17 in place of 1.22 and ended at 125.39, 0.03 ahead of the low columns, and the low half took 1.53 and came 0.24 late for TensorE. f1 gives the 0.31 at the hidden block back. No data came late, but the cover was used up, and the price was paid by the engine beside it. The other items held: the round trip (2.6 for the store; loads 2.9) was in time for groups 2 and 3, and no wait stands in the MLP.
- **The rivals.** (a), the change simply gains, was wrong for the code as made, and right for its idea: e2 and e5 gain as soon as the two tail waits are gone. (b) needed one of them hidden, and neither was. (c), GpSimd's second half ahead of the film products, did not come about: L317 began at 92.59 and 98.39, behind the issue of the second products at 91.96 and 97.76. Its decisive point, a maximum later than 100.8, was badly chosen. It is only where TensorE's cover ends, and the forecast's own 3.3 lies past it too, so after's 101.03 passes it without (c). (d) did not either; e4 shows where it begins.

So in after's trace misses stand on both sides: 0.6 too much in term 4, and in the profiled execution 1.5 for the clock and 0.4 for GpSimd's neighbours that no term had.

**What stays open.** Whether the clock falls is not decided by the wait alone. Executions of one kernel with the same code differ: at 0.993 or lower were 3 of 4 with waits of 2.38 and 1.31 (after), 3 of 4 with 2.25 and 1.31 (f1), 3 of 5 with 2.02 and 1.92 (f2), 5 of 12 with 0.79 and 1.96 (e1), 2 of 6 with 2.25 (s1), and none of 12, 10 and 6 with no wait over 1.31, 1.47 and 0.67 (f3, s2, e5). The waits are those from 120 to 150 us in the one profiled execution of each, and only there is it seen where the clock fell; for the others the mean over the execution is all that is on record. s1 and s2 differ in nothing but the squares and so in the wait, but 6 and 10 executions are few for the chance of a fall. Nor do I know why e4's executions spread from 230.5 to 232.5 in span and e5's from 230.0 to 230.5; the profiled ones differ by 0.4 only, and the medians by 1.1.

## What to carry to other kernels

Work taken off the bound engine gains what it took there, but the work that replaces it is queued somewhere: ask what stands behind it in that queue, and put it where that engine waits anyway (e5: four products in a 1.5 us gap of VectorE, four squares in a gap of ScalarE). When a weight split, or any other long GpSimd instruction, is moved, look at which VectorE instruction it will now run beside, and not only at when its result is wanted. Those slowed most here have two SBUF inputs, but e1's normed rows, with one, took 1.61 instead of 1.14 too. Count a forecast wait of about 2 us on TensorE as more than its length in part of the executions, and look at several executions before reading a loss of 1.5 us from one profile.

## What the runs showed of the hardware that was not expected

- The granted clock fell to 0.50 right after a TensorE wait of about 2 us and stayed there from about 133.5 to 136.9 in after, in some executions and not in others of the same kernel. It makes 24 matmuls of 128x256 take 4.62 in place of 3.11. In the 28 executions of f3, s2 and e5, with no wait over 1.47 here, the mean clock was 0.997 or more. The Trainium skill ("TensorE: Matmul & The Clock Gate", Part 1) says, of the matmuls at a kernel's start, that the number at the lower clock varies from run to run of one kernel. Here it is the stretch behind a wait that varies: 3 of 4 executions of after had the lower mean clock and one had 1.000.
- A coefficient instruction of 128x4 took 1.12 (98.62 to 99.74) beside a GpSimd split that ran from 98.39 to 99.73. The one of 0.45 in the kernel before [rows 6] ended at 102.42, beside one that ended at 102.41, and without such a neighbour it took 0.16 (at 81.23): even the smallest VectorE instruction was held until the other engine's had ended.
- Storing a group's turned rows to DRAM from SP's queue landed in 2.6 us, where ScalarE's stores of turned probabilities took 3.7 in the same trace and 3.4 before [rows 9], though both move 512 KB. Why is not shown.
